# A new instruction order for the state-space stage of a two-layer kernel, with a channel-major time-step projection, two-pass segment sums, and the first block's context product earlier

## The reference, cut to what matters

```
zxbcdt = u @ W_in.T                      # z 512, xBC 640, dt 4 columns
dt = softplus(dt + dt_bias)
xBC = silu(conv4(xBC) + b_conv)          # causal, 4 taps
x_scaled = x * dt;  A_dt = -exp(A_log) * dt
Lmat = exp(segsum(A_dt))                 # within a chunk
Y_diag = (C B^T * Lmat) x_scaled
states = (B * decay)^T x_scaled          # carried from chunk to chunk
Y_off = C states * exp(cumsum(A_dt))
g = (Y + x * D) * silu(z);  y = g * rsqrt(mean(g*g) + eps) * norm_w @ W_out.T
```

## Time and profile before

| what | value |
|---|---|
| median of 3 runs | 1343.14 us (1342.84 to 1344.47) |
| profiled execution | 1342.15 us, of which the span 1340.4 us |
| mean granted TensorE clock | 0.975 |
| PE busy | 1266.9 us (95%) |
| DVE busy | 861.3 us (64%) |
| ACT busy | 609.2 us (45%) |
| POOL busy | 410.9 us (31%) |

### The profile page before, as it was taken

The page is one execution under the profiler, slowest core; times in us unless marked ns, Lnnn a source line. Parts: engine busy times, 40 slices in busy tenths (PEclk is TensorE's granted clock), DMA queues, the critical chain, the costliest instruction groups (busy, mean ns, idle before and its releaser), DMA issues.

```text
span 1340.4 us, 20875 instructions
## 1 busy us (share of the span) xinstructions
PE 1266.9 (95%) x7224; PEld 1057.8 (79%) x7224; DVE 861.3 (64%) x1750; ACT 609.2 (45%) x1125; POOL 410.9 (31%) x536
## 2 busy tenths in 40 slices
PE   6699999999999999999899999999999899999995
PEld 6577888888888888888677667767767688888885
DVE  3487735444453535345576786787686688898996
ACT  3243323232333333233567667677675544444441
POOL 1243400000000000000236655755655334434433
PEclk8899999999999999999899999999999899999997
DMA  4122000101010101000001101100100101010100
GB/s 179 57 79 98 29 4 0 32 1 32 0 32 0 31 0 47 0 16 1 28 1 36 44 11 34 43 23 27 35 24 29 32 17 32 31 31 31 31 16 32
DMA packets 30393, 41.29 MB, mean 31 GB/s; under 512 B 2432, under 2 KB 22912, under 8 KB 30208
## 3 DMA queue, kind: packets, MB, share of 16 engines
q1 hardware_dynamic: 30336, 40.53, 9.3%
HBM read 27.94 MB, written 12.58 MB: 30 GB/s over the span
## 4 chain that ended last, share of the span: by engine, by line
PE 74%; DVE 16%; ACT 5%; issue 4%; POOL 1%; DMA 0%; DVEq 0%; POOLq 0%; ACTq 0%; SPq 0%; PEldq 0%
PE bank L45 22%; PE bank L47 22%; PE bank L46 22%; DVE acc L1145 4%; PE bank L1662 2%; PE bank L1656 2%; DVE mm_ L1226 1%; DVE mag L976 1%; PE bank L1645 1%; DVE state L1244 1%; PE bank L1624 1%; PE bank L1498 1%; DVE wf L984 1%; ACT hh L662 1%; ACT yo L855 1%
## 5 line engine op out<-in xcount | busy, mean ns | idle before, releaser
L1052 DVE TENSOR_TENSOR hb<-gl,bank 128x512 f32<-128x512 f32 x128 | 87.9, 686 | 199.9 <-PE bank L47 197.3
L662 ACT ACTIVATE hh<-hb 128x512 fp32r<-128x512 f32 x128 | 80.9, 632 | 182.4 <-DVE hb L1052 182.4
L701 ACT ACTIVATE gl<-bank 128x512 f32<-128x512 f32 x128 | 76.4, 597 | 181.8 <-PE bank L47 181.7
L1015 DVE TENSOR_TENSOR hl<-hb,hh 128x512 fp32r<-128x512 f32 x128 | 96.1, 751 | 84.5 <-ACT hh L662 84.5
L645 POOL TENSOR_TENSOR dhl<-dab,dhh 128x512 fp32r<-128x512 f32 x64 | 96.2, 1524 | 141.5 <-ACT dhh L662 141.5
L520 POOL TENSOR_TENSOR veb<-mvb,eps 128x4 f32<-128x4 f32 x8 | 1.8, 228 | 378.7 <-DVE mvb L1032 378.7
L45 PE MATMUL bank<-xt_l,w_h 128*128 128x512 f32 x256 | 103.8, 406 | 6.2 <-DVE xt_l L1015 3.4
L45 PE MATMUL bank<-at_l,w_hi_a 128*128 128x512 f32 x256 | 102.8, 401 | 1.2 <-DVE at_l L1015 1.0
L46 PE MATMUL bank<-xt_h,w_l 128*128 128x512 f32 x256 | 102.0, 399 | 0.0
L47 PE MATMUL bank<-xt_h,w_h 128*128 128x512 f32 x256 | 102.0, 398 | 0.0
L47 PE MATMUL bank<-at_h,w_hi_a 128*128 128x512 f32 x256 | 101.7, 397 | 0.0
(11 more groups left out here) (221 smaller groups left out, 3669.0 us busy)
## 6 DMA issues: line engine op xcount, KB each, us to landing
xg<-x_scratch SPq DMA_DIRECT2D x16, 512.0 KB, 3.9
xall<-in_x SPq DMA_DIRECT2D x8, 512.0 KB, 7.8
xg<-in_xt SPq DMA_DIRECT2D x8, 512.0 KB, 4.9
x_scratch<-rows_out SPq DMA_DIRECT2D x8, 512.0 KB, 3.1
x_scratch<-rows_out SPq DMA_DIRECT2D x16, 256.0 KB, 2.2
out<-rows_out SPq DMA_DIRECT2D x8, 512.0 KB, 3.2
wq<-in_codes SPq DMA_DIRECT2D x12, 256.0 KB, 2.6
sc<-in_scales SPq DMA_DIRECT2D x12, 256.0 KB, 2.9
```

The source lines that it names most:

```text
L662: return act.activation(dst, src, ACT.Copy)
L701: act.activation(gl[:, n % 2], ps_gate[n % 2][:], ACT.Gelu_apprx_tanh).then_inc(s_gelu, 1)
L1015: return dve.tensor_tensor(dst, src, hi.bitcast(F32), ALU.subtract)
L1052: dve.tensor_tensor(hb[:, n % 2], gl[:, n % 2], ps_up[n % 2][:], ALU.mult).then_inc(s_h, 1)
```

## The change

* **dt channel-major.** `dt_proj` now makes the last 128 columns of W_in as rows by all 512 tokens, six products of 512 columns. ACT copies them (`dt_keep`, into `dt_rows`), and PE transposes them back in four transposes (`dt_transpose`). `dt_chain` is cut into four pieces that stand apart on DVE.
* **Two-pass segment sums.** POOL splits the rates (`rates_split`) and builds two masked tiles, `au_h` and `au_l`, in place of `au`. Each segment sum is two fp32r products with `below_r` in place of one fp32 product. Of a group's four sums only the first is made in the step before; the other three are made in its own step.
* **x dt by ACT.** ACT writes `xsd`, x times dt, from the same transposed x in PSUM, four activations a chunk (`x_times_dt`). `mm_` is then one DVE instruction a chunk with no scalar, `bw` is weighted by the decay alone, and POOL's `state_weight` goes.
* **One table for Exp and Ln**, loaded by name once a step.
* **New order** on all four engines in a step, with another use of the PSUM banks, and the convolution's last block (B and C) first (`turn`). The copy into `rest` moves to the end of the step on ACT.
* **Start.** `context(0, 0)` and `x1_transpose(0)` move ahead of scores of batch 1, with the ACT and DVE work that they need.

The diff, cut to its core:

```diff
             softmax_transpose(0)
+            context(0, 0)
             scores(GPB)
             scores(GPB + 1)
-            context(0, 0)
+            x1_transpose(0)
             scores(GPB + 2)
             scores(GPB + 3)
-            x1_transpose(0)
...
+                cols = slice(D_IN - P, D_IN)
+                for k in range(KT):
+                    mm = exact3(pe, DT_LANE[:], win_h[:, k, cols], win_l[:, k, cols], xt_h[:, k], xt_l[:, k],
+                                start=k == 0, stop=k == KT - 1)
-                for t in range(NT):
-                    mm = tok_proj(DT_LANE[:, t * HEADS:(t + 1) * HEADS], t, slice(D_IN - HEADS, D_IN))
...
-                pe.matmul(SEG_LANE[t][:], below[:], au[:, t].rearrange("p h l -> p (h l)"),
-                          start=True, stop=True).then_inc(c_seg, 1)
+                pe.matmul(seg_lane(t, more)[:], below_r[:], au_h[:, t].rearrange("p h l -> p (h l)"), start=True, stop=False)
+                pe.matmul(seg_lane(t, more)[:], below_r[:], au_l[:, t].rearrange("p h l -> p (h l)"),
+                          start=False, stop=True).then_inc(c_seg, 1)
...
+                for h in range(HEADS):
+                    x = act.activation(xsd[:, u, h], ps_x[:, h * HEADDIM:(h + 1) * HEADDIM], ACT.Copy,
+                                       scale=dtv[:, b, c, h:h + 1])
...
-                    for h in range(HEADS):
-                        m = dve.scalar_tensor_tensor(mm_[:, u, h], ee[:, c, h], dtv[:, b, c, h:h + 1], small[:, P:2 * P],
-                                                     ALU.mult, ALU.mult)
+                dve.tensor_tensor(mm_[:, u], ee[:, c], small[:, P:2 * P].unsqueeze(1).broadcast_to([P, HEADS, P]),
+                                  ALU.mult).then_inc(c_m, 1)
...
+            def keep_rest(s, b, k):
+                act.wait_ge(c_y3, k + 2 + 1)
+                copy(rest[:], xg[:, b, 2:]).then_inc(c_rest, 1)
...
+                    z_silu(n, 3)
+                    act.preload_act_table_set("natural_log_exp_and_others")
+                    segment_exp(n, 0)
```

More of the change, by code:

```diff
@@ L1127, in _ @@
                 a_lo(0, k)
+            dequant(1)
             score_max(1)
@@ L1176, in project, with dt_done @@
[L1176 to L1188 removed]
+            def dt_done(n, step, ins):
+                ins.then_inc(c_dtc, 1)
+                dve.wait_ge(c_dtc, DT_STEPS * n + step)
@@ L1274, in _ @@
             add_out(GROUPS - 1, 1, last, NT - 1, 1)
+            rows_stats(last, NT - 1)
             def x3_lo(g):
@@ L1491, in _, with x2_transpose @@
                 group(g, True, True, 1)
-            def x2_transpose(n, b, i, place):
+            def x2_transpose(n, b, i, place, between=None):
                 pe.wait_ge(c_xg[b], 16 * (i + 1))
                 for k in range(KT):
+                    if between is not None and k == 1:
+                        between()
+                    if between is not None:
+                        pe.wait_ge(c_zs, NT * n - 1 + k)
                     for t in range(NT):
@@ new lines, in scores_cb, with y_off @@
+            def scores_cb(k, b, c):
+                cols = slice(c * P, (c + 1) * P)
+                pe.wait_ge(c_gm, k + 1)
+                pe.wait_ge(c_bw, k + 1)
+                pe.wait_ge(c_m, k)
+                pe.matmul(small[:, P:2 * P], bc[0:D_STATE, b, cols], ct[:, b, cols], start=True, stop=True)
+                pe.transpose(small[:, 0:D_STATE], bc[0:D_STATE, b, cols],
+                             wide_i[0:D_STATE, P:P + D_STATE]).then_inc(c_G, 1)
+            def y_off(k, b, c):
+                cols = slice(c * P, (c + 1) * P)
+                pe.wait_ge(c_st, k + 1)
+                pe.wait_ge(c_yo, k + 1)
+                pe.wait_ge(c_xtk, k + 1 + 1)
+                pe.wait_ge(c_xsd, k + 1)
+                pe.matmul(ps_yoff[:], ct[:, b, cols], state[:, b].rearrange("p h d -> p (h d)"),
+                          start=True, stop=True).then_inc(c_yoff, 1)
@@ new lines, in state_add, with y_diag @@
+            def state_add(k, u):
+                pe.wait_ge(c_xsd, k + 1)
+                pe.wait_ge(c_bw, k + 1 + 1)
+                for h in range(HEADS):
+                    mm = pe.matmul(ps_ds[0:D_STATE, h * HEADDIM:(h + 1) * HEADDIM], bw[:, u, h], xsd[:, u, h],
+                                   start=True, stop=True)
+                mm.then_inc(c_ds, 1)
+            def y_diag(k, u):
+                pe.wait_ge(c_m, k + 1)
+                pe.wait_ge(c_xsd, k + 1)
+                pe.wait_ge(c_g1, k + 1)
+                for h in range(HEADS):
+                    mm = pe.matmul(ps_y[:, h * HEADDIM:(h + 1) * HEADDIM], mm_[:, u, h], xsd[:, u, h],
+                                   start=True, stop=True)
+                mm.then_inc(c_y, 1)
```

816 lines of the change are left out of this document (495 added, 321 removed).

## The result

| kernel | median, range | ratio to before, 95% interval |
|---|---|---|
| before | 1342.99 us (1342.46 to 1344.47, 4 runs) | |
| changed | 1297.97 us (1295.79 to 1299.41, 4 runs) | 0.9676 [0.9658, 0.9693] |

The profiled execution of the changed kernel took 1298.11 us, its span 1296.2 against 1340.4. The change saves 45 us where 33 were forecast. The measured time lies on the very edge of the forecast range (1298), beside the rival "it all fits" (1299).

The account below looks back on a forecast made before the run. The prediction took PE to set the pace in the state-space steps. Steps -26.8, last step +2.3, hand-over +2 and start -11 sum to -33.5 from 1342.15, giving 1308.6, stated as 1310 us; range 1298 to 1327.

Parts of the forecast that it names:

- it all fits: Rival, 16%: waits of 0.2 us a step, start -12.5, hand-over 0, step 43.1, total 1299 us.
- What bounds the kernel: State-space steps: PE, busy 46.71 of 47.82 us, sets the pace; only its work, clock and waits count.
- PE's work: Each step: dt_proj 0.8 us less, four segment sums 1.55 us less, leaving 42.9 us of work at full clock.
- The clock: Each step: the fall from 2.4 to 1.2 GHz behind dt_proj goes with the four-column products, worth 1.5 us.
- Waits: Each new step: 1.1 us of PE waits, as much as before, ends 0.2 and 3, making the step 44.0.
- near misses: In the step, five places where PE comes within a microsecond of its releaser; each could cost nothing or some tenths.
- Start: Up to the first MLP's first gate, moved from 59.29 to 47 to 51: -11 us, ends 8 and 13.
- Hand-over and first step: State clear ends at 670.3 as before, but PE idles some 5 us and then runs at half pace: +2 us, ends 0 and 4.
- Last step: Three segment sums move in, 1.7 us, plus 0.6 us waiting for `gated1`: +2.3 us.
- POOL holding DVE: Rival, 16%: POOL holds small DVE instructions, convolution and add some 2 us late, step 46, total 1324 us.
- The late load: Rival, 6%: late copy into `rest` delays the next rows' load; a loop of 49.5 us sets the step, total 1348.
- The start that doesn't shift: Rival, 8%: the dequantization chain bounds the first group, so the start's 11 us are given back; total 1321 us.

Follow-up runs that it names:

- dt_channels_old: Kernel before with only dt made channel-major, copied by ACT and transposed back on PE, in the old order: 1345.83 us, ratio 1.0035.
- dt_tokens: Changed kernel with dt made token-major again by 24 four-column products, without the copy and four transposes: 1311.78 us, ratio 0.9793.
- order_only: Changed kernel with both dt token-major and one-pass fp32 segment sums again; new order, x dt by ACT and single table stay: 1325.78 us, ratio 0.9867.
- start_only: Kernel before with only the start's new order, context and x1 transposes ahead of batch 1's scores: 1330.21 us, ratio 0.9924.
- clear_fill: Changed kernel, POOL's state clear earlier in the hand-over; first step's next-row transposes and C B^T ahead of the first product with the state: 1292.47 us, ratio 0.9634.
- after_again: The changed kernel unaltered, run once more for comparison on the chip of the later runs: 1297.65 us, ratio 0.9677.
- keep_warm: clear_fill plus twelve unread 512-column PE products during the hand-over's wait for the first masked tile: 1288.61 us, ratio 0.9606.
- late_load: Changed kernel with one more wait on SP, so the load of the batch's next rows goes out some 2.3 us later: 1312.83 us, ratio 0.9779.

## Why the forecast was right, and where not

* **What bounds the kernel.** This step failed, though the range held. "PE sets the pace there" was read from 46.71 busy of 47.82. dt_channels_old and the second step of before show that a chain over several engines held the old step at 47.5 to 47.8, and that PE's slow stretch behind dt_proj mostly filled waits: without it the step was 0.3 shorter. So dt's lighter form alone (step 47.69) gains nothing in a step, nor did the new order alone in the traced execution (47.92); with the cheaper sums they gain 5.0 together. The two-pass sums in the old order were not run. The forecast, which set one term beside the other, could only hold for the whole change.
* **PE's work.** The sum is right, in part by luck. 42.9 was worked out, 42.80 came. But dt is worth 0.75 for 0.8, and the sums 1.31 for 1.55, since one costs up to 0.65 and not 0.56. The missing 0.3 is work that the prediction did not name: at full clock the old work is 42.80 + 0.75 + 1.31 = 44.86 in the new order, for 45.2 in the old.
* **The clock.** The fall did go, with the products that the prediction named. Its price of 1.5 was no fixed one: 0.3 in the old order, 0 to 4.5 in dt_tokens, 3.1 in order_only.
* **Waits.** The most mis-sized term: 1.1 a step was taken, with 0.2 as the lower end, and it was 0.0. 7 x 1.1 = 7.7 of the 10.7 us by which the sum missed. "As much as before" had no ground: before's waits belonged to the chain of the old order. The laid-out lists had shown no wait; near misses of 0.2 to 0.7 (four are listed, where the prediction counts five) are not waits as long as anything of them is left. One came true to the tenth: y_diag ahead of the first out-projection takes 1.07 for 0.91, 0.16 a step.
* **Start.** -14.4 for -11. The scores of groups 6 and 7 ran at full clock (the gate at 46.23, "46.6 if the clock is high"), 0.8 came from a faster first transfer, and 1.0 more behind the first down-product, where the clock of before fell once more at about 146 us (0.96 from 113 to 158 us) and that of the changed kernel did not. start_only gives 10 of it on its own.
* **Hand-over and first step.** -2.9 for -1.8. POOL's clear was laid to end at 670.3 less the start's shift, 655.9, and ended at 655.4. The half pace behind it was expected at 2; against clear_fill's first step at full clock it is 44.96 - 43.12 = 1.84.
* **Last step.** +2.26 for +2.3, with another split: PE's busy time rose by 1.3 (37.24 for 35.95) where 1.7 was laid, and its waits are 1.0 for 0.6.
* **Rest.** +1.5 that no step of the prediction had. From the last step's end to the row below it is 24.00 us, for 22.75 before (1041.36 to 1064.11), so most of it lies there, and PE's wait for the low part of x3 is 4.33 us for 2.81:

```profile
1019.62 0.76 PE L45 MATMUL bank<-xt_l,w_h 128*128 128x512 f32 x1 [4.33 <-DVE xt_l L1122]
```

  Not tested. The same wait is 4.34 in after_again, 2.88 in clear_fill and 2.82 in keep_warm; the cause is open.
* **Rivals.** POOL holding DVE: the mechanism is there, and in the new order the price is not. The instruction of the earlier trace rows, on which the prediction weighed it, now takes

```profile
L1286 DVE SCALAR_TENSOR_TENSOR adt<-dtv,a x8: 174/174/176, 645.6 to 934.7; 128x16 f32<-128x16 f32 x8
L1276 DVE TENSOR_TENSOR dm<-de,drec x8: 174/1086/1091, 644.7 to 931.3; 128x16 f32<-128x16 f32 x8
```

  176 ns at most, but its neighbour is held in most of its eight executions. "Seven of eight were not held" said nothing on the new place of the others, and the one that was held had already cost the kernel before a step of 48.90. 1.8 us a step are lost on DVE so (much of the 2.9 by which its 37.0 exceeds the 34.1 laid), the room ahead of `gt_l`, 1.8 and not the 0.7 laid, absorbs it, and PE loses at most 0.16, not 2. The late load: not reached, with 0.9 us of room; in late_load, where it is, the clock nearly doubles its price (15.5 us for 8.7 of waits). The start that doesn't shift: excluded by start_only.

## What to carry over

PE busy at 98% of a step, with a clock below full in it, doesn't show that PE bounds the step: look for a step of the same kernel in which the clock did not fall. If it is nearly as long (47.5 for 47.8 here), another chain holds the period, and lighter PE work gains little until the order lets the chain shrink too. Cut such steps at one and the same instruction: a window of before that began at the product with the state and ended at the next C B^T would be 1.1 us too short. Lay the new lists out and price the waits from them, not from those of the old order. Where a list has to wait for a first clear or a first tile, put other ready work ahead of the waiting instruction: here 5 us of clock and wait for a few moved lines. Look at every small DVE instruction that the new order puts beside a long POOL one.

## What the runs showed of the chip

* TensorE's clock fell with no idle PE at all: behind 24 four-column products PE was busy for 16.94 of 16.94 us at a mean clock of 0.70, and for 16.72 of 16.72 at 0.90 in another step of the same run. With six 512-column products in their place it stayed at 1.00 in the changed kernel's steady steps. In the old order it still fell in three of seven steps with them, behind waits of 0.84 and 0.67 us for other engines, and did not in the other four, which have the same waits.
* A wait of 1.4 us was followed by 7.56 us at 0.55 of the full clock (nearly all of it at 1.2 GHz) in one step and by none of it in others; behind the same wait of 2.9 us in the hand-over the next transposes ran at half pace in one trace and at full pace in three. The same program has it or not.
* POOL's two-input instructions of 1.0 to 1.3 us hold DVE instructions of 16 columns to their own end: 0.17 becomes 0.96 to 1.33 in every step of the changed kernel (`dden`), and once in seven steps of the kernel before (`adt`, 1.27), by where the order puts them.
